# A graph network's merge of layer one: the second bias added on TensorE, the norm read from PSUM, ELU's clamp on ScalarE, and the last norm's offset added to x one layer earlier

## The reference, cut to what matters

```python
_layer_norm = lambda x, g, b: (x - mu) * rsqrt(var + eps) * g + b
h_local = elu((agg + x.reshape(n, NH, FOUT)).reshape(n, NH * FOUT) + gat_b)
h_local = _layer_norm(h_local, ln_local_g, ln_local_b)
y = _mamba(x[perm], ...)
h_attn = _layer_norm(x + y[inv], ln_global_g, ln_global_b)
gate = sigmoid(h_local @ wl.T + h_attn @ wg.T)
h = gate * h_local + (1.0 - gate) * h_attn
ff = relu(h @ ff1_w.T + ff1_b) @ ff2_w.T + ff2_b
return _layer_norm(h + ff, ln2_g, ln2_b)      # layer one's result
...
x = x + layer_one(h)
h = maximum(_layernorm(x), 0)                 # goes into layer two
```

## Time and profile before

| | |
|---|---|
| median of 3 runs | 7670.6 us (7658.32 to 7676.65) |
| profiled execution | 7664.3 us |
| its span | 7662.5 us |
| `close_and_project` in the span | about 2690 to 3035 us |
| `merge` with its loads | about 4799 to 5229 us |
| behind it (`finish`) | about 5229 to 7662 us |

### The profile page before, as it was taken

One profiled execution on the slowest core, in us unless ns is written; L12 is line 12 of the kernel. 1 busy time (PEld: TensorE's weight loads), 2 busy tenths in 40 slices (PEclk: granted clock), 3 DMA queues, 4 the chain that ended last, 5 costly groups with the idle time before them and its releaser, 6 DMA issues. The chain is left out here.

```text
span 7662.5 us, 93224 instructions
## 1 busy us (share of the span) xinstructions
PE 5301.7 (69%) x20089; PEld 3402.6 (44%) x20089; DVE 5059.9 (66%) x10755; ACT 3288.3 (43%) x11052; POOL 4403.2 (57%) x4270
## 2 busy tenths in 40 slices
PE   4756788888888734757777776686666665655565
PEld 4623344444444423224444443574444443444443
DVE  7677588888888754559999996674555553333332
ACT  1124466666666622768898996461000000000000
POOL 2150156566666445037777774425777775777775
PEclk9988899999999955869999998897888786888887
DMA  5114388888888765258999998324555556555556
GB/s 200 19 66 108 136 274 276 273 283 277 282 276 277 209 214 165 88 205 323 319 330 321 324 316 213 113 85 144 175 182 175 182 175 128 171 165 171 165 171 135
DMA packets 546591, 1554.18 MB, mean 203 GB/s; under 512 B 135295, under 2 KB 248587, under 8 KB 530666
## 3 DMA queue, kind: packets, MB, share of 16 engines
q0 software_dynamic: 234128, 827.21, 36.3%
q1 hardware_dynamic: 276540, 691.01, 25.4%
q10 hardware_dynamic: 35516, 31.49, 1.3%
HBM read 1183.69 MB, written 593.47 MB: 232 GB/s over the span
## 5 line engine op out<-in xcount | busy, mean ns | idle before, releaser
L1263 POOL DMA_INDIRECT rows_e<-hidden,unit_src x1856 | 1767.1, 952 | 627.5 <-issue 543.3
L618 POOL DMA_INDIRECT rows_e<-table,unit_src x928 | 1034.1, 1114 | 848.0 <-PE acc_e L823 446.0
L1000 POOL DMA_INDIRECT rows_e<-table,unit_src x928 | 1059.6, 1142 | 375.4 <-issue 270.5
L1291 DVE SCALAR_TENSOR_TENSOR sums_e<-sums_e,unit_keep,acc_e 128x256 f32<-128x256 f32 x928 | 444.9, 479 | 1215.1 <-PE acc_e L1372 1214.1
L1372 PE MATMUL acc_e<-rows_e,same 128*128 128x256 f32 x1856 | 719.4, 550 | 643.6 <-DMA rows_e<-hidden,unit_src 629.1
L812 ACT ACTIVATE rows_e<-rows_e 128x64 f32<-128x64 f32 x4640 | 1119.0, 333 | 1.9
L1084 ACT ACTIVATE rows_e<-rows_e 128x64 f32<-128x64 f32 x3712 | 919.9, 333 | 3.8
L1416 ACT ACTIVATE turned_f<-turn_f 128x512 f32<-128x512 f32 x98 | 58.5, 597 | 1886.5 <-PE turn_f L1388 1886.5
L1372 PEld LDWEIGHTS acc_e<-rows_e,same 128*128 128x128 f32 x1856 | 491.5, 281 | 828.8 <-DMA rows_e<-hidden,unit_src 695.6
L823 PE MATMUL acc_e<-rows_e,unit_w 128*128 128x512 f32 (+1 forms) x1856 | 710.3, 530 | 144.7 <-DVE rows_e L805 102.7
L1372 PE MATMUL acc_e<-rows_e,links 128*128 128x256 f32 x1856 | 522.9, 431 | 323.3 <-DMA rows_e<-hidden,unit_src 322.9
(11 more groups left out here) (474 smaller groups left out, 9341.4 us busy)
## 6 DMA issues: line engine op xcount, KB each, us to landing
bc<-bc_rows SPq DMA_DIRECT2D x228, 896.0 KB, 5.6
summed<-sums_e SPq DMA_DIRECT2D x464, 390.0 KB
staged<-sums_e SPq DMA_DIRECT2D x116, 1024.0 KB, 4.6
summed<-sums_e SPq DMA_DIRECT2D x464, 130.5 KB
rows_e<-table,unit_src POOLq DMA_INDIRECT x1856, 5.3
hots<-hot_e SPq DMA_DIRECT2D x116, 256.0 KB, 5.0
hots<-unit_w SPq DMA_DIRECT2D x116, 256.0 KB, 4.7
rows_e<-hidden,unit_src POOLq DMA_INDIRECT x1856, 2.8
```

The source lines that it names most:

```text
L618: pool.indirect_dma_start(self.rows[:, v, e, :], None, table, bass.IndirectOffsetOnAxis(unit_src[:, u, e:e + 1], 0)).then_inc(self.landed[ ...
L1000: pool.indirect_dma_start(self.rows[:, v, e, :], None, self.tab, bass.IndirectOffsetOnAxis(unit_src[:, u, e:e + 1], 0)).then_inc(self.land ...
L1263: pool.indirect_dma_start(self.rows[:, v, e, :], None, tab, bass.IndirectOffsetOnAxis(unit_src[:, u, e:e + 1], 0)).then_inc(self.landed[v ...
L1291: dve.scalar_tensor_tensor(self.sums[:, at_, :], self.sums[:, (n - 1) % self.SUMS, :], unit_keep[:, u:u + 1], self.acc[:, n % self.ACCS, 0 ...
```

## The change

Four edits. In `merge`, step 11's `min(l, 0)` on DVE becomes `relu(-l)` on ACT, and the exponential takes a scale of -1. `ff2_b` is added by one more product for each block in step 37 (a row of ones as 1 x 128 weights, the bias as a 1 x 256 moving row), step 38 is gone, and the norm reads its input from PSUM: bn_stats on DVE and the scaling on ACT. The norm's offset, old step 46, is gone, and with it the load of `ln2_b`; a job now has 52 steps. In `close_and_project` the offset is added to x on DVE, into a part of `r3` that is free by then, and that sum is what goes to `x_dram`; this add is issued in the turn of the norm's bn_stats, ahead of them. One more broadcast load stands at the start of that stage.

```diff
 def layer_norm(ch, x3, out3, stat, relu=False, gain=None):
     if gain is not None:
         yield ch.step(dve, lambda: dve.tensor_tensor(out3, out3, bc(gain), ALU.mult))
-        yield ch.step(dve, lambda: dve.tensor_tensor(out3, out3, bc(shift), ALU.add))
...
+            offset, ld_offset = broadcast(lsb, "offset", a["L1_gnn_ln2_b"])
+            chain.dma(sp, ld, ld_offset,
...
 # close_and_project
                     yield ch.step(dve, lambda: dve.tensor_tensor(x3, x3, part[0], ALU.add))
+                    ch.apart((dve, lambda: dve.tensor_tensor(part[1], x3, offset[:, :].unsqueeze(1).broadcast_to([P, m, D]), ALU.add)))
                     yield from layer_norm(ch, x3, t3, stat[:, k, :, :], relu=True)
-                    yield ch.move(lambda e: e.dma_start(blk(x_dram), x3), lambda e: e.dma_start(blk(h_dram), t3))
+                    yield ch.move(lambda e: e.dma_start(blk(x_dram), part[1]), lambda e: e.dma_start(blk(h_dram), t3))
...
-        names = ("gat_b", "ln2_g", "ln2_b", "ff2_b")
+        names = ("gat_b", "ln2_g", "ff2_b")
...
 # merge
-                yield ch.step(dve, lambda: dve.tensor_scalar(t3, l3, 0.0, None, ALU.min))
+                yield ch.step(act, lambda: act.activation(t3, l3, ACT.Relu, scale=-1.0))
                 dve.wait_ge(returned[b0 // PART_OF], 16 * min(PART_OF, T - b0 // PART_OF * PART_OF))
-                yield ch.apart((act, lambda: act.activation(t3, t3, ACT.Exp)),
+                yield ch.apart((act, lambda: act.activation(t3, t3, ACT.Exp, scale=-1.0)),
...
+                                    [lambda b=b: pe.matmul(o_ps[:, b, :], ones[0:1, :], vecs["ff2_b"][0:1, :],
+                                                           start=False, stop=False, skip_group_check=True)] +
...
-                yield ch.step(dve, lambda: dve.tensor_tensor(l3, o_ps[:, 0:m, :], bv("ff2_b"), ALU.add))
-                yield from layer_norm(ch, l3, l3, st, gain=vecs["ln2_g"][:, :], shift=vecs["ln2_b"][:, :])
+                yield from layer_norm(ch, o_ps[:, 0:m, :], l3, st, gain=vecs["ln2_g"][:, :])
```

More of the change, by code:

```diff
@@ L478, in draw_own, with layer_norm @@
                                                                      .rearrange("p u h -> p h u"), own_ps[:, :, 0:n], ACT.Copy))
-        def layer_norm(ch, x3, out3, stat, relu=False, gain=None, shift=None):
+        def layer_norm(ch, x3, out3, stat, relu=False, gain=None):
             g = x3.shape[1]
@@ L1993, in graph_stack_kernel @@
             chain.step(dve, lambda: dve.memset(low[:, :], -BIG))
-            chain.dma(sp, ld,
+            offset, ld_offset = broadcast(lsb, "offset", a["L1_gnn_ln2_b"])
+            chain.dma(sp, ld, ld_offset,
                       *[lambda k=k, v=v: sp.dma_start(att[:, k, :], v.rearrange("h d -> (h d)").partition_broadcast(P))
```

## The result

The changed kernel takes 7757.16 us (median of 4, 7752.97 to 7761.34) against 7667.93 us: ratio 1.0117, 95% interval 1.0099 to 1.0134. That is 89 us more, where 74 were forecast; the time lies in the range of 7690 to 7790.

The account below looks back on a forecast made before the run. The merge was taken as bound by a loop through PE and a short stretch of ACT's queue. 39 + 8 - 6 - 2 + 21 - 1 + 1 + 16 gave +76 us on 7664.3, taken as 7742, range 7690 to 7790.

Parts of the forecast that it names:

- The loop through PE and ACT's stretch: Merge, per job: PE runs 11.5 us, waits 2.6 for step 36's relu behind ACT's queue, plus 0.6: 14.7 us.
- The turns: Merge: lanes return after 55 turns, not 57; ACT work between relus of steps 34 and 36 is 93 us against 54: +39.
- The product: Step 37 in the merge: added bias product at 0.43 us a block, 49 blocks, all on PE's path: +21 us.
- DVE's relief: Merge: DVE loses 44.5 us of 293, which gives nothing because DVE is not in the loop.
- The norm from PSUM: Merge: at most 2 us of ACT gained, none taken; reads on DVE 0, bounds 0 and 3 us, off the loop.
- The clock: Merge: PE falls to the lower clock in lanes 5 and 6, 6 jobs, 16 us; lanes 2 to 4 taken as 0.
- The closing: close_and_project: 25 adds, 17 us of DVE, mostly covered by waits for POOL; 1 us with the extra load.
- The small terms (8, -6, -2 and -1): Work ahead of step 34 +8 us, PE work in the longer gap -6, last jobs without neighbours -2, the ends -1.
- only the product: Rival, merge: the stall stays 2.6 us and the change costs PE's 21 us: 7690; chance 0.08.
- DVE as the bound: Rival, merge: the loop is DVE's after all, so its relief gains, -30 us: 7640; chance 0.06.
- That the clock holds: Rival, merge: queues as counted but PE's clock does not fall, +60 us: 7726; within the main case's 0.82.

Follow-up runs that it names:

- scaling_later: Kernel before with a blank turn ahead of the norm's scaling and a lane's next job one turn earlier, still 57 turns; ratio 0.9971.
- turns_only: Kernel before with all its instructions, but steps 38 and 46 without turns of their own, so a lane comes round after 55 turns; ratio 1.0047.
- no_product: Changed kernel without the product for the bias, ff2_b left out of the computation, all turns kept; ratio 1.0057 against the kernel before.
- closing_alone: Kernel before with the last norm's offset added in the closing, step 46's work and the load gone, a blank turn for step 46; ratio 1.0019.
- offset_alone: Kernel before with the last norm's offset added in the closing, step 46 and the load gone, no blank turn; ratio 1.0047.
- relu_alone: Kernel before with only ELU's clamp on DVE made relu(-l) on ACT, turns as before; ratio 1.0006.
- turns_only_filled: turns_only with four products into a bank nothing reads, issued on PE in step 36's turn; ratio 1.0031 against the kernel before.

## Why the prediction was right, step by step

**The loop through PE and ACT's stretch: right.** The even spacing of about 14.7 us turned uneven, as it should. scaling_later shortened the loop from the other side, by 24 us where 20 were counted. One sign came out otherwise: the spacing should have been shortest after lane 0 and longest after lanes 5 and 6. The longest (23.3 us) does follow lane 5, but the shortest (14.1) follows lane 6, since the stretch of the job that a spacing leads to, here lane 0's, goes into it. PE was to be busy below 85%: it was 83.0 and 84.8 in the windows shown, but 88.8 from 5100 to 5200 us.

**The turns: mechanism right, term mis-sized.** 39 us more were counted for the stretch on ACT; it grew by 20.5 (54.3 to 74.8). Lane by lane it is 1.62, 2.31, 3.28, 3.47, 3.46, 4.36 and 4.37 us, where 1.70, 2.78, 3.86, 4.14, 4.14, 5.15 and 5.15 were counted. The list of instructions was right, their prices weren't: a pair of activations shown as 1.09 us starts its successor after 0.99 to 1.00, and the longer the list, the more of that adds up. This makes 14 us; the last four jobs, which lack neighbours, make another 4, where 2 were taken off. Before, the count came out right, 54, because in some jobs a wait for DVE (0.27 us ahead of step 44) filled what the overlap saves: a job has 2.08 us there, or 2.46, not 2.17 in each. turns_only says the same: 27 counted, 16.5 measured, and the clock beside it.

**The product: mechanism right, term mis-sized.** That one row of weights instead of 128 saves nothing in the load held (197 ns), but the switch to one row and back costs 0.39 us a block on top of 0.43. 21 us predicted, 40 by the timeline, 47 by no_product in the change's turns. This error of 19 us and the one of 18 in the turns go opposite ways and nearly cancel.

**DVE's relief: right.** closing_alone takes 17 us of DVE work out of the merge, and it stays as long (431.3 against 429.6); offset_alone takes out the same and is 45 us longer.

**The norm from PSUM: right.** 7 ns more for bn_stats, 35 less for ACT's scaling. The 65 ns estimated from the Trainium skill (VectorE: DVE Perf Modes, section on the TRN2 errata) don't show in this instruction either.

**The clock: mechanism right, but not which jobs.** A fall in each of the six jobs of lanes 5 and 6 was predicted, 16 us; for lanes 2 to 4 the bounds were 0 and 29 us, and 0 was taken. Read job by job from PE's timeline, step 37 took more than its 6.1 us in ten jobs, by 0.9 to 3.9 us, 22 us in all, 9 or 10 of them in lanes 5 and 6 and 12 in lanes 2 to 4. It is in lane 5 all three, in lane 6 one of three, in lane 3 the first three, in lane 2 two, in lane 4 one. In lanes 2 and 3 PE's longest idle pieces ahead of step 37 were 1.74 and 1.92 us, with shorter ones around them; one job of lane 2 needed 9.4 us for step 37. Yet the same idle pieces did not always bring a fall. This is ahead of step 37 of a job of lane 4:

```profile
5075.47 0.66 PE L2537 MATMUL bank<-ident,hl 128*128 128x128 f32 x4 [2.44 <-ACT hl L2536]
```

The first four records of step 37 behind these 2.44 us took 1.03 us, full clock. In the round before, the same 2.44 us in lane 4 were followed by four records of 1.92 us. So which jobs are hit isn't explained by the length of the idle piece. The Trainium skill (TensorE: Matmul & The Clock Gate, HAM oscillation) describes waits between groups of products, there for a DMA, that send the clock back each time. The windows of this trace, with 0.91 to 0.95, agree that waits send it back, but here they don't do it each time.

**The closing: 1 us predicted, about 5 measured** by the means of the first ten profiles (8.6 from before to after alone), with a spread between profiles of the same size, and nothing among the last three. So it isn't shown for certain that the closing costs anything; ten or more, the sign of being wrong, is not what the means show. DVE's wait for POOL went from 95.0 to 88.8 us, so only 6 of the 17 us of adds were taken out of that wait. Where the other 11 went, and whether they are on the path, is open.

**The sum: near, in part by luck.** In the merge the stretch on ACT (20.5), the product (40) and the clock (22) make 83 of the 87 us; 39, 21 and 16 were predicted. The small terms (8, -6, -2 and -1) weren't measured one by one, and 4 us are left for them. That 7742 came so near to 7757 owes something to two errors that cancel.

The rivals: only the product (7690) falls with turns_only; DVE as the bound falls with closing_alone and relu_alone. That the clock holds falls with the windows.

## What to carry to other kernels

Where several jobs are interleaved in fixed turns through in-order queues, an instruction's price is not its length alone. It depends on which other instructions then stand between two dependent ones of the bounding engine, and removing a step can cost more than adding one. Look for the stretch in which the busiest engine waits, list what stands in the other engine's queue there, and move that by a blank turn: one turn was worth 0.3% here, two lost ones cost 0.5%. A bias by a product with one row of weights was paid nearly twice over here, 0.82 us instead of 0.43, because its neighbours use all rows.

## What the runs showed of the hardware

- A float32 product of 256 columns with one row of weights between products of 128 rows took 0.82 us, the same with 128 rows of ones 0.43 us; the weight loader stood idle 0.33 us ahead of each switch.
- PE's clock fell after an idle piece of 1.74 us with shorter ones and short products around it, as well as after one of 3.4, but in other jobs not after 2.44 and 2.49. A fall made step 37 of the changed kernel 0.9 to 3.9 us longer. In turns_only_filled 1.7 us of products that nobody needs, put into the gap, kept it at 1.00 in the windows, and the merge was 17 us shorter than turns_only's.
- Of two ACT instructions with no wait between them the second starts about 0.1 us before the shown end of the first (a pair of 1.09 us is followed after 0.98 to 1.00).
